# A cross-attention kernel on one core: two products per Gram block made one of 512 columns, with an addition on VectorE

## The reference

```python
g_x     = conv1x1(g_w, g_b, x_2).transpose(0, 2, 1)        # x_2 is ctx
theta_x = conv1x1(theta_w, theta_b, x).transpose(0, 2, 1)
phi_x   = conv1x1(phi_w, phi_b, x_2)
W  = einsum('bnc,bcm->bnm', theta_x, phi_x) / 1024
y  = einsum('bnm,bmc->bnc', W, g_x).transpose(0, 2, 1)
wy = conv1x1(w_w, w_b, y)
wy = bn_gamma * (wy - bn_mean) * rsqrt(bn_var + 1e-5) + bn_beta
return wy + x
```

## Time and profile before

| | before |
|---|---|
| median of 3 runs | 752.22 us (752.21 to 752.46) |
| the profiled execution | 752.43 us, span 750.6 us |
| TensorE busy | 742.9 us, 99%, 3810 products |
| VectorE busy | 578.1 us, 77% |
| ScalarE busy | 479.1 us, 64% |
| GpSimd busy | 353.9 us, 47% |

### The profile page before, as it was taken

How to read it: one execution, slowest core, us unless ns; L and a number is a source line. 1 busy time by engine, 2 the same in 40 slices (tenths; PEclk the granted TensorE clock), 3 DMA queues, 4 the chain that set the end, 5 groups by cost and what they waited for, 6 DMA issues and landing times.

```text
span 750.6 us, 12963 instructions
## 1 busy us (share of the span) xinstructions
PE 742.9 (99%) x3810; PEld 639.7 (85%) x3810; DVE 578.1 (77%) x1416; ACT 479.1 (64%) x1281; POOL 353.9 (47%) x272
## 2 busy tenths in 40 slices
PE   7999999999999999999999999999999999999998
PEld 6688988889888888988889888888888889888886
DVE  3887878868787787878868787787877868787685
ACT  4676775756767575775756857576775756857341
POOL 6957253472715528153472625628154472624600
PEclk9999999999999999999999999999999999999999
DMA  9828374281834708365181733708355181740202
GB/s 271 195 104 224 113 160 178 46 250 42 197 140 84 251 0 224 112 137 198 35 242 58 193 142 76 259 0 224 112 118 218 29 227 79 174 163 1 113 0 113
DMA packets 87100, 103.21 MB, mean 138 GB/s; under 512 B 3466, under 2 KB 69924, under 8 KB 87076
## 3 DMA queue, kind: packets, MB, share of 16 engines
q1 hardware_dynamic: 84944, 101.86, 47.1%
q10 hardware_dynamic: 2132, 1.05, 0.7%
HBM read 69.35 MB, written 33.55 MB: 137 GB/s over the span
## 4 chain that ended last, share of the span: by engine, by line
PE 98%; DMA 1%; POOL 0%; DVE 0%; ACTq 0%; ACT 0%; issue 0%; POOLq 0%
PE wbank L900 51%; PE gbank L900 46%; PE wbank L946 1%; DMA ctx_sb<-in_ctx_dram 1%; PE wbank L924 0%; PE wbank L952 0%; POOL ctxT_lo L366 0%; PE wbank L936 0%; DVE ctxT L646 0%; PE wbank L1080 0%; ACT ctxT_hi L450 0%; ACTq L492 0%; DVE x_sb L879 0%; ACTq L181 0%; PE wbank L911 0%
## 5 line engine op out<-in xcount | busy, mean ns | idle before, releaser
L366 POOL TENSOR_TENSOR ctxT_lo<-ctxT,ctxT_hi 128x512 fp32r<-128x512 f32 x124 | 160.6, 1324 | 350.1 <-ACT ctxT_hi L450 350.1
L423 POOL TENSOR_TENSOR x_lo<-x_sb,x_hi 128x1024 fp32r<-128x1024 f32 x60 | 142.4, 2400 | 0.0
L890 DVE SCALAR_TENSOR_TENSOR x_sb<-wbank,const,x_sb 128x512 f32<-128x512 f32 x110 | 77.5, 747 | 70.0 <-PE wbank L900 70.0
L556 ACT ACTIVATE mt<-stage 32x224 fp32r<-32x224 f32 (+1 forms) x210 | 70.3, 335 | 95.3 <-DVE stage L692 90.9
L473 ACT ACTIVATE room<-ctx_sb 128x256 f32<-128x256 f32 x240 | 96.3, 403 | 32.2 <-DMA ctx_sb<-in_ctx_dram 26.3
L900 PE MATMUL gbank<-ctxT_lo,ctxT_hi 128*128 128x512 f32 x360 | 84.0, 389 | 0.0
L900 PE MATMUL gbank<-z_hi,mt 128*128 128x512 f32 x256 | 81.6, 390 | 0.0
L646 DVE STREAM_TRANSPOSE ctxT<-ctx_sb 128x512 f32<-128x512 f32 x124 | 78.7, 682 | 2.7 <-DMA ctx_sb<-in_ctx_dram 2.6
L900 PE MATMUL wbank<-x_hi,wt_hi 128*128 128x512 f32 x256 | 79.7, 392 | 0.0
L900 PEld LDWEIGHTS gbank<-ctxT_lo,ctxT_hi 128*128 128x128 f32 x360 | 67.6, 188 | 14.0
L900 PE MATMUL wbank<-x_lo,wt_hi 128*128 128x512 f32 x256 | 79.0, 390 | 0.0
(11 more groups left out here) (138 smaller groups left out, 1544.8 us busy)
## 6 DMA issues: line engine op xcount, KB each, us to landing
x_sb<-in_x_dram SPq DMA_DIRECT2D x16, 2048.0 KB, 7.8
out_dram<-x_sb SPq DMA_DIRECT2D x63, 512.0 KB, 2.8
ctx_sb<-in_ctx_dram SPq DMA_DIRECT2D x124, 256.0 KB, 4.7
ctx_sb<-in_ctx_dram ACTq DMA_DIRECT2D x4, 256.0 KB, 7.1
x_sb<-in_L_xattn_w_w_dram SPq DMA_DIRECT2D x1, 512.0 KB, 9.2
stage<-in_L_xattn_theta_w_dram SPq DMA_DIRECT2D x1, 512.0 KB, 14.4
phi_nat<-in_L_xattn_phi_w_dram SPq DMA_DIRECT2D x1, 512.0 KB, 13.6
x_sb<-in_L_xattn_g_w_dram SPq DMA_DIRECT2D x1, 512.0 KB, 14.1
```

Source lines behind the costliest of these rows:

```text
L366: nc.gpsimd.tensor_tensor(ctxT_lo[:, c, :], turned_ctx(b, c), f(ctxT_hi[:, c, :]), ALU.subtract).then_inc(sem_, 1)
L423: nc.gpsimd.tensor_tensor(x_lo[:, k, :], x_sb[par][:, k, :], f(x_hi[:, k, :]), ALU.subtract).then_inc(x_lo_made, 1)
L556: return nc.scalar.activation(dst, src, ACT.Copy)
L890: nc.vector.scalar_tensor_tensor(out=x_sb[par][:, m, cols], in0=OUT_BANK[m][h][:, :], scalar=const[:, m:m + 1], in1=x_sb[par][:, m, cols], ...
```

## The change

`wp_hi` and `wp_lo`, the high and low part of phi's weights, now lie side by side in one tile `wp` (512 columns). In `t_block` the products of a Gram block's high part with `wp_hi` and with `wp_lo`, both summed into the same 256 columns of a bank, become one product with all 512 columns of `wp`, into the whole bank: high by high is summed in its left half, high by low in its right half. The product of the low part with `wp_hi` stays and goes to the left half. VectorE then takes the left half as before (L830, in the new text L832), with a new semaphore `t_half`, and adds the right half to `stage` in a new instruction, which waits for the first and raises `t_taken`.

```diff
--- before.py
+++ after.py
@@ -110,8 +110,9 @@
         q_lo = sb("q_lo", [P, KI, C], F32R)
         wt_hi = sb("wt_hi", [P, KC, CI], F32R)
         wt_lo = sb("wt_lo", [P, KC, CI], F32R)
-        wp_hi = sb("wp_hi", [P, KC, CI], F32R)
-        wp_lo = sb("wp_lo", [P, KC, CI], F32R)
+
+        wp = sb("wp", [P, KC, 2 * CI], F32R)
+        wp_hi, wp_lo = wp[:, :, 0:CI], wp[:, :, CI:2 * CI]
         z_hi = sb("z_hi", [P, KC, C], F32R)
         z_lo = sb("z_lo", [P, KC, C], F32R)
         phi_nat = sb("phi_nat", [P, KI, C])
@@ -248,6 +249,7 @@
         low_done, low_hi_made, low_lo_made = (sem(n) for n in ("low_done", "low_hi_made", "low_lo_made"))
         s_done, s_made, s_taken = (sem(n) for n in ("s_done", "s_made", "s_taken"))
         th_done, th_hi_made, th_lo_made = (sem(n) for n in ("th_done", "th_hi_made", "th_lo_made"))
+        t_half = sem("t_half")
         t_done, t_taken, t_hi_made, t_lo_made = (sem(n) for n in ("t_done", "t_taken", "t_hi_made", "t_lo_made"))
         q_done, q_taken, q_hi_made, q_lo_made = (sem(n) for n in ("q_done", "q_taken", "q_hi_made", "q_lo_made"))
         work_free = sem("work_free")
@@ -830,7 +832,10 @@
                     nc.vector.scalar_tensor_tensor(out=stage[:, r * CI:(r + 1) * CI], in0=bp_row[:, :],
                                                    scalar=s_col[:, m:m + 1],
                                                    in1=gbank[T_BANK[r]][:, 0:CI],
-                                                   op0=ALU.mult, op1=ALU.add).then_inc(t_taken, 1)
+                                                   op0=ALU.mult, op1=ALU.add).then_inc(t_half, 1)
+                    dve.wait_ge(t_half, KC * b + (r + 1))
+                    nc.vector.tensor_tensor(stage[:, r * CI:(r + 1) * CI], stage[:, r * CI:(r + 1) * CI],
+                                            gbank[T_BANK[r]][:, CI:2 * CI], ALU.add).then_inc(t_taken, 1)
                     if r > 0:
                         t_lo_part(r - 1)
                 t_lo_part(KC - 1)
@@ -1057,15 +1062,14 @@
                 def t_block(r):
 
                     m = T_ORDER[r]
-                    dst = gbank[T_BANK[r]][:, 0:CI]
+                    dst = gbank[T_BANK[r]]
                     order = sorted(range(KC), key=lambda j: (j, m) not in HELD)
                     for n, j in enumerate(order):
                         if (j, m) not in HELD and (order[n - 1], m) in HELD:
                             pe.wait_ge(low_lo_made, 2 * b + (1 if r < 2 else 2))
                         g_h, g_l = gram_block(gram_hi, low_hi, j, m), gram_block(gram_lo, low_lo, j, m)
-                        mm(dst, g_h, wp_hi[:, j, :], n == 0, False)
-                        mm(dst, g_h, wp_lo[:, j, :], False, False)
-                        ins = mm(dst, g_l, wp_hi[:, j, :], False, n == KC - 1)
+                        mm(dst[:, :], g_h, wp[:, j, :], n == 0, False)
+                        ins = mm(dst[:, 0:CI], g_l, wp_hi[:, j, :], False, n == KC - 1)
                     ins.then_inc(t_done, 1)
 
                 if first(b):
```

## The result

The changed kernel takes 759.87 us (759.67 to 760.34, 4 runs), the kernel before 752.31 us (752.21 to 752.46, 4 runs). The ratio is 1.0099, with a 95% interval of 1.0087 to 1.0112: 1% slower. The profiled execution has a span of 758.5 us, against 750.6 before. The forecast was 760.1, from 750.4 to 761.8.

The account below looks back on a forecast made before the run. TensorE was taken to bound the kernel, with 98% of the span. Twelve batches losing 0.61 us, two losing 0.48 and two gaining 0.19 gave +7.9, so 760.1 us from a 752.22 median; range 750.4 to 761.8.

Parts of the forecast that it names:

- What bounds the kernel: Whole kernel: TensorE holds 98% of the span, so only its products and the waits before them change the time.
- The additions: VectorE after each L830 in T: 0.41 us each, four a batch, 1.8 us more queue; by lengths alone all fits.
- t_lo(0) and GpSimd: T's first low part on VectorE lands 0.08 us behind GpSimd's fourth ctxT_lo and waits until 1.17 after that start.
- The price per batch: Q, after T, runs as if 0.61 us later in twelve batches, bounds 0.49 and 0.71, T's saving included.
- the restart: TensorE at Q's start after a wait: first products slower, 1.20 us instead of 1.10 for four.
- The 0.2133 for a pair: T's products: bound where a pair costs only its columns, no fixed part, 0.2133 us instead of 0.2396.
- the rival that the pair saves nothing: T's products: merging two into one 512-column product saves no time; 763.1 us, or 753.5 with t_lo(0) first; chance 0.03.
- The saving of T: T's products: 0.0117 us saved per pair, 16 times a batch, 0.19 us a batch, 3.0 us in 16.
- The first batch: Theta's products stand between T and Q there, so it only gains 0.19 us, perhaps less some hundredths.
- The fourth block's wait: TensorE in T waits for the first t_taken; in the first batch little room, perhaps some hundredths of a us.
- The second batch: GpSimd stands some 0.13 us earlier against T, so t_lo(0) is late for certain and the loss is 0.48.
- the twelve alike batches: Batches where GpSimd stands against T as in the seventh, which was read; each loses 0.61 us.

Follow-up runs that it names:

- GpSimd waits: The changed kernel, with GpSimd starting its fourth ctxT_lo only after the four low parts of T; 750.67 us, ratio 0.9982.
- additions only: The changed kernel with three products of 256 columns per Gram block as before, VectorE's additions kept; 760.89 us, ratio 1.011.
- GpSimd in halves: The changed kernel with GpSimd's fourth ctxT_lo cut in two instructions of 256 columns, no new wait; 752.90 us, ratio 0.9999.
- low part first: The changed kernel with VectorE, from T's second block on, doing the previous block's low part between L832 and the addition; 756.77 us, ratio 1.0052.
- low parts after: The changed kernel with T's first two low parts moved behind the third addition on VectorE; 755.13 us, ratio 1.0027.
- grouped: The changed kernel with GpSimd's wait, each block of T doing its four 512-column products first, then the four of 256; 750.01 us, ratio 0.9963.

## Why the prediction was right

- **What bounds the kernel.** TensorE, and every loss through a wait in front of it: borne out by the chain.
- **The additions.** 0.41 was taken, 0.42 measured (L837), with 0.04 from L832's end to its start and 0.34 to the instruction behind. They disturb nothing by their length (GpSimd waits: 750.67).
- **t_lo(0) and GpSimd.** It was computed to start 0.08 behind GpSimd's fourth ctxT_lo and starts 0.10 behind. The wait was to end 1.17 after GpSimd's start, and ends 1.14 after it. That who starts first goes first was an inference from two rows of 1.12 and 0.62; the second batches of the changed kernel and of the additions only show it within 0.12 us, on both sides. The 0.03 ahead in the kernel with GpSimd's instruction in halves falls on the same side. The Trainium skill, "SBUF — State Buffer", section Who interferes with whom, says that a VectorE instruction with at most one SBUF input doesn't contend with GpSimd, outside the modes in which VectorE uses both of its ports. The trace agrees for the new addition, one input in SBUF and one in PSUM: it keeps its 0.42 (321.67) while ctxT_lo runs beside it.
- **The price per batch.** 0.61 forecast, 0.62 measured. Q's first product was to come 321.84 - 315.58 = 6.26 into T and comes at 6.23; the restart was put at 0.10, from TensorE's first products behind a wait, and costs 0.14, of which 0.11 is the late weight load.
- **Two sums of the prediction don't come out.** The 0.2133 for a pair isn't what the two spacings give, which is 2 x 0.1081 = 0.2162; nothing was taken from it. And the rival that the pair saves nothing was priced at 763.1, with 0.19 more in every batch. But where GpSimd sets Q's start, T's length doesn't count, as the prediction itself says of the saving: this rival gives 12 x 0.61 + 2 x 0.48 = 8.3, thus 760.5, and the additions only, where the pair does save nothing, took 760.89.

Three terms were off. The saving itself hardly counts in the sum, since it is used only where nothing waits; the errors of the first two batches nearly cancel:

- **The saving of T** was mis-sized: 0.0117 a pair from Q's spacing, measured (5.75 - 5.64) / 16 = 0.0069. 16 x 0.11 = 1.8 us instead of 3.0. The nearest row for a 512-column product had its like beside it, and this one doesn't; the prediction named that gap and put nothing on it. Its 0.2279 was the mean of two paces in Q: the first five products behind T take 0.232 each (321.33 to 322.49), the other nineteen 0.227 (to 326.80).
- **The first batch** was to gain 0.19 and loses 0.27 (from T to the next T 48.43, was 48.16). The fourth block's wait, put at some hundredths, makes its first product 0.21 late behind the one before it (spacing 0.21 instead of 0.12, and the next 0.33 behind that instead of 0.23), and later the output's products have a gap of 0.32 and one of 0.31 instead of 0.23. The wait in T isn't in every execution: in the kernels with GpSimd waits, low part first and GpSimd in halves T takes 5.86 in the first batch, here and with the low parts after 6.03 and 6.04. The rows of the changed kernel:

```profile
45.65 0.28 PE L905 MATMUL gbank<-wp,low_lo 128*128 128x256 f32 x1
45.86 0.50 PE L905 MATMUL gbank<-wp,gram_hi 128*128 128x512 f32 x1
...
60.80 0.39 PE L905 MATMUL gbank<-th_hi,q_lo 128*128 128x512 f32 x1
61.12 0.70 PE L905 MATMUL wbank<-th_hi,q_hi 128*128 128x512 f32 x2
```

- **The second batch** was to lose 0.48, "late for certain", and gains 0.11 (45.10 to the next T): GpSimd's fourth ctxT_lo, which had stood at 93.14 - 89.51 = 3.63 into T, stands at 93.70 - 89.76 = 3.94. That step took GpSimd's place against T as fixed. It holds for the twelve alike batches, not for this one, which follows the first and its other delays. What comes ahead of it is later too: ScalarE's first ctxT_hi by 0.56 (88.67, now 89.23) and VectorE's additions of the Gram rows by 0.55 (81.07, now 81.62), while T starts only 0.25 later. From where VectorE is late there was not followed further.

By the measured parts: 0.27 - 0.11 + 0.58 + 0.61 (the third and fourth) + 10 x 0.62 + 0.47 (the fifteenth, 45.68) - 0.12 (the last, 28.03, was 28.15) = 7.9, as between the two spans; the medians are 7.6 apart. The forecast sum was 7.9 as well, with errors of -0.46 in the first batch, +0.59 in the second and -0.1 in the others together. The mechanism and its price carried it. That the first two batches cancel was luck.

## What to carry to other kernels

An instruction is added to an engine with idle time in front of it, and the idle time is enough; what counts as well is which later instruction it pushes past whose start. Before putting work in a gap, list what on that engine excludes another engine (here VectorE instructions with two inputs in SBUF against GpSimd's), and ask on which side of the other's start each one lands afterwards. Where it lands badly, moving the engine with slack is the cheap remedy: one wait on GpSimd turned 1% slower into 0.2% faster.

## What the runs showed of the hardware

- A VectorE instruction with two SBUF inputs (a low part) and a GpSimd one with the same (ctxT_lo) exclude each other until the first is nearly over. A start 0.03 or 0.07 ahead won, one 0.05 behind lost. VectorE got in 1.14 to 1.17 us after GpSimd's start with 512 columns and 0.61 after it with 256; the longest wait in these rows is 1.11 (1.53 instead of 0.42).
- A wait in front of TensorE costs more than the pause, for the weight load waits too. With a pause of 0.59 us before Q, Q's 24 products took 0.14 us more (5.61 against 5.47, in other batches 5.57 to 5.62), at a granted clock of 1.00; with 0.03 us (GpSimd in halves) about the same, 45.24 - 45.10 - 0.03 = 0.11; with 0.21 us before it (low parts after) only 0.05 in most batches. There the load is noted at 322.37, 0.03 ahead of the product; what makes the rest of the difference isn't shown.
- A 512-column product between 256-column ones costs more than among its like: T takes 5.64 in turns, 5.59 grouped (with Q behind it at 5.49 instead of 5.47), 5.56 by the spacings of the kernel before.
